# Second attention step: level flags gathered on TensorE, a new order on GpSimd and SyncE, and R tiles one pair ahead

## What is computed

```python
def top_p(X):
    logits = (X @ W1.T @ W2.T) @ (X @ W3.T).T        # 4096 x 4096
    probs = softmax(logits, axis=-1)
    # keep the largest probabilities of each row until their sum reaches 0.9
    A = probs * mask
    return A / A.sum(-1, keepdims=True)

R = adj + I;  R = R / R.sum(-1, keepdims=True)
Xf = Xa = X;  Z = 0
for n in range(2):
    A = top_p(Xa)
    Xf = R @ Xf
    Xa = A @ Xa
    Z = Z + Xf @ U1[n].T + Xa @ U2[n].T
out = layernorm(X + layernorm(X + Z) * ln_g + ln_b)
```

## Time and profile before

| | us |
|---|---|
| median of 3 runs | 4336.78 (4332.68 to 4336.88) |
| profiled execution, its own time | 4337.12 |
| its span | 4335.3 |
| TensorE busy | 3723.9 (86%) |
| VectorE busy | 3619.4 (83%) |
| ScalarE busy | 3108.2 (72%) |
| GpSimd busy | 1179.7 (27%) |

### The profile page before, as it was taken

One profiled execution on the slowest core, in us unless ns is written; L12 is line 12 of the kernel. 1 busy time (PEld: TensorE's weight loads), 2 busy tenths in 40 slices (PEclk: granted clock), 3 DMA queues, 4 the chain that ended last, 5 costly groups with the idle time before them and its releaser, 6 DMA issues.

```text
span 4335.3 us, 66096 instructions
## 1 busy us (share of the span) xinstructions
PE 3723.9 (86%) x25236; PEld 3136.2 (72%) x25236; DVE 3619.4 (83%) x6399; ACT 3108.2 (72%) x3129; POOL 1179.7 (27%) x1476
## 2 busy tenths in 40 slices
PE   8677877777777769999999759999999998889886
PEld 5677777777777747777777548888887877667665
DVE  2999999999999939888888199999999877787775
ACT  3788889898988855555555378888888766776661
POOL 0000000000000000101001145555555565566565
PEclk9899999999999989999999879999999999999888
DMA  3211111111111020000000213322233323322332
GB/s 118 92 47 64 45 59 53 47 64 47 64 46 66 27 71 12 19 16 18 17 16 18 73 45 99 100 93 93 94 107 116 121 79 105 102 89 79 106 98 75
DMA packets 131760, 292.49 MB, mean 67 GB/s; under 512 B 14123, under 2 KB 94187, under 8 KB 127059
## 3 DMA queue, kind: packets, MB, share of 16 engines
q1 hardware_dynamic: 131410, 287.99, 20.1%
HBM read 250.19 MB, written 37.75 MB: 66 GB/s over the span
## 4 chain that ended last, share of the span: by engine, by line
PE 34%; ACT 31%; issue 16%; POOL 14%; DVE 3%; DMA 1%; SPq 0%; ACTq 0%; POOLq 0%; DVEq 0%
PE ps L810 11%; PE ps L653 9%; ACT b L881 7%; ACT b L1000 7%; ACT b L1001 7%; ACT b L875 3%; POOL b L479 3%; PE ps L799 3%; PE ps L755 3%; PE ps L634 2%; POOL b L476 2%; POOL b L482 2%; ACT b L981 2%; ACT b L869 1%; POOL b L543 1%
## 5 line engine op out<-in xcount | busy, mean ns | idle before, releaser
L714 PE MATMUL ps<-b 128*128 128x257 f32 x4096 | 927.6, 387 | 114.2 <-DMA b<-in_adjTb 105.2
L714 PEld LDWEIGHTS ps<-b 128*128 128x128 f32 x4096 | 790.9, 194 | 244.6 <-DMA b<-in_adjTb 110.7
L810 PE MATMUL ps<-b 128*128 128x257 f32 x4096 | 901.2, 379 | 0.0
L653 PE MATMUL ps<-cb,b 128*128 128x128 f32 x4096 | 606.2, 312 | 321.8 <-ACT b L875 321.8
L810 PEld LDWEIGHTS ps<-b 128*128 128x128 f32 x4096 | 770.8, 189 | 111.4
L653 PEld LDWEIGHTS ps<-cb,b 128*128 128x128 f32 x4096 | 546.1, 163 | 371.3 <-ACT b L875 329.5
L1161 DVE SCALAR_TENSOR_TENSOR b<-b 128x4096 f32<-128x4096 f32 x128 | 566.5, 4426 | 61.7 <-ACT b L869 58.2
L1163 DVE CUSTOM_DVE_ANT_0 b<-b 128x4096 f32<-128x4096 f32 x128 | 566.4, 4425 | 5.7 <-DMA b<-in_adj 1.3
L881 ACT ACTIVATE b<-ps 128x1024 f32<-128x1024 f32 x512 | 499.8, 1022 | 73.7 <-PE ps L653 72.6
L634 PE MATMUL ps<-b 128*64 128x128 f32 x8192 | 503.5, 276 | 0.0
L875 ACT ACTIVATE b<-b 128x4096 f32<-128x4096 f32 x128 | 474.4, 3706 | 8.2 <-DVE b L1165 8.2
(11 more groups left out here) (184 smaller groups left out, 4854.0 us busy)
## 6 DMA issues: line engine op xcount, KB each, us to landing
b<-in_adjTb SPq DMA_DIRECT2D x256, 512.0 KB, 3.7
b<-in_adj SPq DMA_DIRECT2D x32, 2048.0 KB, 8.1
y_d<-b SPq DMA_DIRECT2D x64, 128.0 KB, 1.7
h_d<-b SPq DMA_DIRECT2D x64, 128.0 KB, 1.8
b<-h_d SPq DMA_DIRECT2D x64, 128.0 KB, 2.2
b<-in_xT SPq DMA_DIRECT2D x1, 4096.0 KB, 15.5
b<-in_x SPq DMA_DIRECT2D x32, 128.0 KB, 2.2
b<-y_d SPq DMA_DIRECT2D x32, 128.0 KB, 2.0
```

The lines of the kernel that those rows point to most:

```text
L653: last = nc.tensor.transpose(bank(2 * (gq % 3), 2)[:, b * 128:(b + 1) * 128], ub[:, u % UB, j * 128:(j + 1) * 128], ident_s)
L714: last = mm(b[:, 0:XA], aj[:, q % AJR, e, :], xf[:, j, :], start=(j == 0), stop=(j == NT - 1))
L810: last = mm(o[:, 0:XA], at[:, q % ATR, b, :], xa[:, j, :], start=(j == 0), stop=(j == NT - 1))
```

## The change

- `RLEAD` becomes 1: `pairs_in(n)` gives pair n+1 to round n (pair 1 to round 0, none to round 31). The `+ 2` in `fslot` keeps every slot's round as it was.
- The level flags of s = 1: VectorE links the last flag, reduces the five columns of `lev` to one (`lev1`) and raises `lv`. TensorE waits for `lv` and multiplies `lev1` (one column as weights) with the identity into row 0 of a PSUM slot (`gather_level`), between the two R tiles of the round (in rounds 0 and 31 at the end). VectorE's `finish` waits for that and reduces the 128 flags from PSUM. ScalarE doesn't read the slot; it counts it as free after its third level.
- GpSimd in s = 1 has no `levels`; its new order is r_post, final_second, final_first, final_add, scale_a, accumulate, bracket.
- SyncE: the stores of the R tiles and the load of `gx` (`rstore`) go between the chunks of the first tile of the pair and those of the second; only in the round of pair HT do they come ahead of the `xf` reload.
- `levat` gives the count of slots at which the flags of a tile are there.

```diff
--- before.py
+++ after.py
@@ -45,9 +45,9 @@
     NQ = N // 512
     HT = NT // 2
     CT = 4
-    RLEAD = 0
-
-    fslot = {max(HT + m - RLEAD + 1, 2 * m + 4): m for m in range(HT)}
+    RLEAD = 1
+
+    fslot = {max(HT + m - RLEAD + 2, 2 * m + 4): m for m in range(HT)}
     LAST = max(fslot)
 
     def pairs_in(n):
@@ -168,6 +168,7 @@
         iota = r1.take(16)
         lev = r1.take(5)
         levr = r1.take(5)
+        lev1 = r1.take(1)
         levi = r1.take(1).bitcast(I32)
         w8 = r1.take(3, 8)
         zE = r1.take(3)
@@ -386,20 +387,23 @@
                     for i in range(2):
                         ld(gxi[:, i, :], tile_of(gx_d, 2 * p + i), g["gi"])
 
-            def adjpairs(n):
+            def adjpairs(n, half):
                 for p in pairs_in(n):
-                    for q in range(2 * p * NCH, 2 * (p + 1) * NCH):
+                    for q in range((2 * p + half) * NCH, (2 * p + half + 1) * NCH):
                         adjchunk(q + AJR)
 
-            gxload(0)
-            adjpairs(-1)
-            for n in range(LAST + 4):
-                for p in pairs_in(n - 1):
+            def rstore(n):
+                for p in pairs_in(n):
                     for i in range(2):
                         r = 2 * p + i
                         sp.wait_ge(g["yd"], r + 1)
                         ld(tile_of(y_d if r < NT else z_d, r % NT), yr[:, i, :], g["ys"])
                     gxload(p + 1)
+
+            gxload(0)
+            adjpairs(-1, 0)
+            adjpairs(-1, 1)
+            for n in range(LAST + 4):
                 if 3 <= n < NT + 3:
                     sp.wait_ge(g["acc"], n - 2)
                     ld(tile_of(h_d, n - 3), hh, g["nz"])
@@ -426,10 +430,14 @@
                         ld(finz[:, i, :], tile_of(z_d, r), g["fi"])
                         ld(finx[:, r % 4, :], tile_of(X_d, r), g["fi"])
                 if HT in pairs_in(n):
+                    rstore(n - 1)
                     sp.wait_ge(g["ys"], 16 * NT)
                     sp.wait_ge(g["R"], NT * NCH)
                     chunked(xf, y_d)
-                adjpairs(n)
+                adjpairs(n, 0)
+                if HT not in pairs_in(n):
+                    rstore(n - 1)
+                adjpairs(n, 1)
             sp.wait_ge(g["fd"], 16 * NT)
             barrier(sp, kS[1])
 
@@ -563,21 +571,18 @@
                     if s == 1:
                         for p in pairs_in(n - 1):
                             r_post(p)
+                        if n - 2 in fslot:
+                            final_second(fslot[n - 2])
+                        if n - 1 in fslot:
+                            final_first(fslot[n - 1])
+                        if n in fslot:
+                            final_add(fslot[n])
                     if 1 <= n <= NT:
                         scale_a(n - 1)
                     if 2 <= n <= NT + 1:
                         accumulate(n - 2)
-                    if s == 1:
-                        if n - 2 in fslot:
-                            final_second(fslot[n - 2])
-                        if n - 1 in fslot:
-                            final_first(fslot[n - 1])
-                        if n < NT:
-                            levels(n)
-                        if n in fslot:
-                            final_add(fslot[n])
-                        if n + 2 < NT:
-                            bracket(n + 2)
+                    if s == 1 and n + 2 < NT:
+                        bracket(n + 2)
                 barrier(po, kS[s])
 
         @block.tensor
@@ -811,6 +816,10 @@
                                       start=(j == 0), stop=(j == NT - 1))
                         last.then_inc(g["av"], 1)
 
+                def gather_level(t):
+                    pe.wait_ge(g["lv"], t + 1)
+                    mm(lslot()[0:1, 0:128], lev1, ident_s, start=True, stop=True).then_inc(g["pl"], 1)
+
                 for t in range(2):
                     mq(None, t, zx(None, t))
                     if s == 0:
@@ -840,7 +849,11 @@
                     if s == 1:
                         for p in pairs_in(n):
                             Rmul(2 * p)
+                            if n >= 1:
+                                gather_level(n)
                             Rmul(2 * p + 1)
+                        if n == 0 or n == NT - 1:
+                            gather_level(n)
                 barrier(pe, kS[s])
 
         @block.scalar
@@ -1048,6 +1061,9 @@
                                 av_ev(n - 1)
                             if n >= 2 or n + 3 < NT:
                                 mq_ev(n - 2 if n >= 2 else None, n + 3 if n + 3 < NT else None)
+                    if n < NT:
+                        lc[0] += 1
+                        ac.sem_inc(g["el"], 1)
                     for r in items[:1]:
                         r_ev(r)
                     if n + 2 < NT:
@@ -1305,7 +1321,8 @@
                     if s == 0:
                         v.tensor_scalar(lev[:, 3:4], nt_, r_, None, ALU.is_gt).then_inc(g["lv"], 1)
                     else:
-                        v.tensor_scalar(lev[:, 3:4], part, 8.5, None, ALU.is_ge).then_inc(g["lv"], 1)
+                        link(v.tensor_scalar(lev[:, 3:4], part, 8.5, None, ALU.is_ge))
+                        v.tensor_reduce(lev1, lev, AX.X, ALU.max).then_inc(g["lv"], 1)
 
                 def mark(sync, t, j):
                     io = iota[:, 8 * j:8 * j + 8]
@@ -1355,8 +1372,13 @@
                         mark(link, t, 0)
                         if t + 2 < NT:
                             rmax(t + 2)
-                    ve.wait_ge(g["lr"], t + 1)
-                    link(v.tensor_reduce(levi[0:1, :], levr[0:1, :], AX.X, ALU.max))
+                    if s == 0:
+                        ve.wait_ge(g["lr"], t + 1)
+                        flags = levr[0:1, :]
+                    else:
+                        ve.wait_ge(g["pl"], levat[t])
+                        flags = bank(2 * ((levat[t] - 1) % 3))[0:1, 0:128]
+                    link(v.tensor_reduce(levi[0:1, :], flags, AX.X, ALU.max))
                     level = ve.value_load(levi[0:1, :], min_val=0, max_val=2)
                     with ve.If(level >= 1):
                         if s == 0:
@@ -1376,12 +1398,16 @@
                 if s == 1:
                     el_at += 2 + NL // 2
                     eat[1] = el_at
-                for n in range(NT - 1 - s):
-                    el_at += NL // 2 + (NCH if n >= 1 else 0)
-                    eat[n + 1 + s] = el_at
+                levat = {}
+                for n in range(NT):
+                    el_at += NCH if n >= 1 else 0
+                    if n + 1 + s < NT:
+                        el_at += NL // 2
+                        eat[n + 1 + s] = el_at
                     tx = n + 2 + s < NT
                     el_at += 2 if (n >= 2 or tx) else 0
-                    el_at += 1 if (s == 0 and tx) else 0
+                    el_at += 1 if (s == 1 or tx) else 0
+                    levat[n] = el_at
                 if s == 0:
                     cmax(0)
                 else:
```

## The result

| | before | after |
|---|---|---|
| median of the runs side by side, us | 4335.19 (4332.68 to 4336.88) | 4236.43 (4235.33 to 4238.58) |
| ratio after to before, 95% interval | | 0.977 (0.976 to 0.979) |
| span of the profiled execution, us | 4335.3 | 4235.1 |
| TensorE busy, us | 3723.9 | 3719.9 |
| VectorE busy, us | 3619.4 | 3636.8 |

The change saves 98.8 us. I had predicted 4233.2. No engine works much less: what went is idle time. In the kernel after, L821 is the flag matmul, L804 `Tr`, L719 the R tiles, L1381 VectorE's flag reduction, L1392 the mask, L1325 the reduction to `lev1`, L484 to L503 bracket, with L492 the value that ScalarE's first level waits for.

What follows compares the result with a forecast made beforehand. No engine full; waits rooted in GpSimd's level turn bound late rounds. Late rounds 53.55 + 0.45 + 0.7 = 54.7, early 51.0, plus reload and end, gave 4231.4, a saving of 103.9: 4233.2 us, range 4208 to 4278.

Steps and rivals of the forecast that it cites:

- The root: GpSimd's level turn, claimed as root of VectorE's flag wait and TensorE's 9.7 us chunk gap in late rounds.
- Flag matmul: TensorE, between the two R tiles: 0.25 us, bounds 0.1 and 1.0, +3.5 us over 14 early rounds.
- Reload: TensorE's gap as the xf reload moves from round 16 to 15: 4.9 us, bounds 0 and 9.
- The clock term: TensorE in the reload round: 1.0 us added for the lower clock behind a gap.
- Contention: Final chain on GpSimd beside VectorE's threshold: threshold instructions slowed, +0.7 us a late round.
- Rival A: VectorE and GpSimd in each other's way: ten threshold instructions lose 0.4 us each, 4276; chance 0.12.
- Flags on VectorE: Linked step and small reduction (+0.3), 128 flags read from PSUM instead of 5 (+0.15): +0.45 us a round.
- lv wait: TensorE at the flag matmul in late rounds, waiting 1.3 us for VectorE's raised flag.
- Bracket: Bracket's chain on GpSimd, starting 6 us earlier, meets the same VectorE passes; given no gain.
- Rival B: ScalarE's level chain becomes the bound if a fourth VectorE pass stops bracket: +3.9 in 12 rounds, 4280; chance 0.08.
- End: Rounds 30 and 31: 49.2 and 50.3 without VectorE's wait, 1.15 more each; then 52.4 us to the end.
- Rivals C and D: C: SyncE meets an overlooked wait, late rounds near 60, 4297, chance 0.06; D: late r_post starves TensorE, 4473, chance 0.04.

## Why the prediction was right, and where it was not

*The forecast.* VectorE bounds late rounds once its wait is gone: right, 54.72 against 54.7. It is the term that carries the gain, and it didn't need the reason that I gave for the wait. That it came out to 0.02 us is luck, as its two additions missed in opposite directions: the flags added 0.1 net instead of 0.45, the contention 1.07 instead of 0.7.

*The root.* I wrote that both waits have one root, the level turn, and that the chunk gap "goes in each late round" as if that were part of the gain. The first is half the story, the second is no gain. The loop of GpSimd and ScalarE bound the round; the turn was 14.1 of its 62 us, and the final chain's place another 7.5. Either edit alone breaks it (4231.3 and 4247.8), and SyncE's order with the lead brings nothing alone (4339.8). With the loop gone the latter is worth 5 us by the medians: 4226.1 with it, 4231.3 without. With SyncE's order and RLEAD as in the change the four kernels are (medians in us; turn and final chain by GpSimd's order):

| | old order on GpSimd | new order on GpSimd |
|---|---|---|
| turn on GpSimd | 4339.8 | 4243.7 |
| turn on TensorE | 4226.1 | 4236.4 |

With the turn gone the new order is not a help but a cost of 10 us. A forecast by parts, each credited with the waits that it removes, would have summed these gains twice. Mine came out because I counted the bound that is next, and counted it once.

*Flag matmul.* 0.50 us instead of 0.25 in 14 rounds, inside the bounds of 0.1 and 1.0. L821 stands between the R tiles in an early round:

```profile
3261.55 0.38 PE L821 MATMUL ps<-cb,b 128*1 128x128 f32 x2
...
3275.88 3.65 PE L804 MATMUL ps<-cb,b 128*128 128x128 f32 x32
```

Tr(14) starts at 3275.88, 3.3 later than my 3272.6; that is this term, 14 x 0.25.

*Reload.* The gap is 4.43, against 4.9:

```profile
3303.41 17.12 PE L719 MATMUL ps<-b 128*128 128x257 f32 x64 [4.43 <-DMA b<-y_d]
...
3334.80 3.65 PE L804 MATMUL ps<-cb,b 128*128 128x128 f32 x32
```

The clock term was mis-sized: the first tile behind the gap took 17.12 instead of 14.08, at a granted clock of 0.82 over 18 us, so 3.0 where I took 1.0 from the pair of before, which lost 1.6 (29.59 against 28.0, at a granted clock of 0.90 over its first 14 us). The round took 58.92 instead of 57.0, which puts Tr(15) 5.2 behind my 3329.6.

*Into the late rounds.* Mask 17 is done at 3423.43 + 5.8 = 3429.2, 5.3 late. Mask 18 is 3482.1, against 3475.5, 1.3 more, since the 54.7 us round is nearly reached there already (3476.26 - 3423.43 = 52.83). The eleven rounds that follow add 601.9, against 601.7.

*Contention.* The size was right (0.7 forecast, 1.07 measured against the old order), the instructions were not. I named L1283 and L1287; of these, now L1299 and L1303, the medians stayed at 0.27 and 0.20. (In the kernel with GpSimd's order alone their medians are 0.71 and 0.64: there they lie beside other instructions of GpSimd.) Hit were two one-element instructions with two tensors, the mark of 8 columns and a whole pass. Rival A's condition, that many small instructions are hit as well, came true for a few only. Of the four rows above, L1309, L1315 and L1271 read two tensors. L1330, of the mark, reads one, and it went from 0.281 to 0.774 all the same, so one input, half of what I had against rival A, did not keep an instruction clear. What tells the instructions that are hit from the others is not shown.

*Flags on VectorE.* Forecast +0.45: the reduction from PSUM takes 0.27 instead of 0.15 and the linked `lev1` adds about 0.3. But the kernel with the flags alone takes 53.65 a round, 0.1 above the 53.55 that I started from. The new work itself is near the forecast: from round 21 to 22 of that kernel the reduction takes 0.12 more, and the link and `lev1` 0.19, 0.3 in all. The rest is contention that moved as GpSimd did: the mask takes 0.22 more, but L1249 of before falls from 4.48 and 4.92 to 4.58 and 4.49, and L1313 from 0.54 to 0.28.

*lv wait.* 1.5 us at the flag matmul in late rounds, against 1.3.

*Bracket.* "No gain" was wrong. Timeline of GpSimd in the changed kernel:

```profile
3700.13 0.75 POOL L484 TENSOR_SCALAR b<-b 128x1 f32<-128x1 f32 x1 [12.11 <-ACTq L1003]
...
3701.41 4.30 POOL L487 TENSOR_SCALAR b<-b 128x1 f32<-128x1 f32 x1
...
3711.25 0.57 POOL L492 TENSOR_TENSOR b<-b,cb 128x1 f32<-128x1 f32 x1
```

The old L484 ends at T+11.1 (T = 3700.8), 6.3 earlier, and ScalarE's idle before its levels falls from 8.22 to 1.88. It lies off the path in the changed kernel, so the sum didn't feel it; in the kernel before it was on it. Rival B was thereby further off than I gave it.

*End.* Rounds 30 and 31 took 50.1 and 48.4, 98.5 in all, against 101.8. Round 30 is as forecast (50.35), round 31 is 3.0 shorter (51.45). In the kernel before, VectorE lost some 2 us of round 31 beside GpSimd (one pass at 4.92, L1252 at 0.62, L1283 and L1287 at 0.65 and 0.64); the changed kernel has these at 4.49, 0.22, 0.27 and 0.20, and I had added contention there instead of taking it away. The last `Tr` and what follows it:

```profile
4182.71 5.63 PE L804 MATMUL ps<-cb,b 128*128 128x128 f32 x32 [10.45 <-DVE b L1392]
```

4235.1 - 4182.7 = 52.4, as forecast. The sum of the errors: +3.3 (matmul), +1.9 (reload), +1.4 (to mask 18), +0.2, -3.3 (end) = +3.5, and the median is 3.2 above the forecast, the profiled execution (4236.94) 3.7. So nearly half of what had been missed up to mask 18 was given back by chance at the end. One slip in the bounds changes nothing: flags and contention can add 0.45 + 0.6 = 1.05 a round, not 1.2, which makes the forecast's own upper end 4262.

*RLEAD and SyncE.* RLEAD at nothing is right to within a few us, and no run shows it closer: the first gap fell from 42 to 9.4 us, and no gain of that size came of it. That its last chunk behind the first y stores costs "a few us" was right only with SyncE's new order; with the old one it is 18 us, and overruns the slack. Rivals C and D: the z stores stand at 3738.32, 11 us behind the first of the four chunks, and no gap follows.

## What to carry to other kernels

Before an edit is credited with a wait, follow the chain of one round in order of time: the largest waits of the two busiest engines were here slack beside a loop of the two others, and one of them could be removed whole for nothing. If two edits break the same loop, the gain is the distance to the next bound, once, and an edit that moves work into a wait gains at most that wait (here 7.5 of 14.8 us). Test each alone, as the second may be pure cost (here 10 us). The place of a step in its engine's queue, ahead of or behind the one that waits, can be worth nearly as much as the step itself: moving some calls on GpSimd was worth 87 us, and taking the level turn off it 105.

## What was not expected of the hardware

- Some of GpSimd's one-element instructions are held up by VectorE's passes over 4096 columns: in the changed kernel three of bracket in a late round (L487, L490, L493) take 4.3 to 4.6 us, as long as such a pass, and not 0.2 to 0.6. L487 above runs from 3701.41 to 3705.71, and beside it on VectorE a pass from 3701.07 to 3705.56:

```profile
3701.07 4.49 DVE L1265 SCALAR_TENSOR_TENSOR b<-b 128x4096 f32<-128x4096 f32 x1
```

- The other way round, a VectorE pass of 4.48 us beside GpSimd's instructions of 256 or 257 columns takes 4.9 to 5.0 (L1271 in the changed kernel 4.94, L1393 in the one with GpSimd's order back 5.00), and a 128x1 instruction with two tensors 0.69 instead of 0.16 (L1330 with the statistics interleaved, L1316 with GpSimd's order back). Shortening a block by 1.3 us gave back half of it (late rounds 54.72 to 54.10), as other instructions then fell beside GpSimd's.
- One `partition_all_reduce` holds GpSimd for 13 to 14 us in a late round (some 6 before and 7 to 8 behind its 0.39 us row): 14.1 in the kernel before, 13.2 with GpSimd's order alone, 13.8 with the all-reduce back.
- A one-column matmul between two R tiles cost 0.50 us of TensorE in an early round (51.27 against 50.77), a second one behind it 0.22 (51.49).
- TensorE, at a granted clock of 1.00 until it idled 4.43 us for the reload (3280 to 3300), came back at a mean of 0.82 over the next 18 us, and its first R tile took 17.12 us instead of 14.08. From 3303 to 3307 the granted clock was 0.50, from 3307 to 3311 it was 0.69, and from 3311 on 1.00.
